# Softmax sums of four heads in one group of matmuls, reciprocals spread by DMA, packed narrow weights, and an output stored batch by batch

## The chip, the cores and the metric

The kernel runs on one core of a Trainium2 chip. Five engines work side by side and meet at semaphores: TensorE (PE), VectorE (DVE), ScalarE (ACT), GpSimd (POOL) and SyncE (SP), which here issues nearly all DMAs. The metric is the time of one execution on the device in microseconds (us); lower is better.

## The reference

Eight layers in a row work on x, 4 batches of 512 tokens with 320 features. In order: a self-attention and a cross-attention with 20 heads of width 64 (inner width 1280) and a gated feed-forward of width 1280; the same three with heads of width 16; a small gated attention; and one more cross-attention with heads of width 16. All is float32. The piece that matters here:

```python
scores = jnp.einsum('bhnd,bhmd->bhnm', q, k) * SCALE
attn = jax.nn.softmax(scores, axis=-1)
out = jnp.einsum('bhnm,bhmd->bhnd', attn, v)
out = out.transpose(0, 2, 1, 3).reshape(B, N, HEADS * DHEAD)
return jnp.einsum('bnf,fe->bne', out, wo) + bo
```

## The kernel before

x stays in SBUF from the first load to the last store. Each engine runs its own instruction list, in program order; what stands on one engine waits for another by semaphores only. The order of work is written out by hand as turns.

**The wide attentions** (`WideRun`, stages 0 and 1) are 8 batches of 10 steps. A step U = 10 n + u handles pair u of heads, two heads of width 64. TensorE computes for it the scores by key block (L491), subtracts the row maxima (L500), computes the bf16 rows of the next step for its maxima (L513), the projections Q and K of the step after the next (`w_QK_first`, `w_QK_rest`, L625 to L635), then `mix` (L574: probabilities times values, the two heads beside each other in 64 columns of the array each) and `den` (L589: the sum of the probabilities over all keys, spread over 64 rows for each head by a stationary block of ones). Before `den`, GpSimd has added the four key blocks of probabilities into `psum` (L556, L560). ScalarE copies `den` out of PSUM into the tile `ox` (L596), VectorE takes the reciprocals in four slices into `rec` (L603) and multiplies the unnormalised output `OT` by it (L609). Every so often a step has more work on TensorE: the output projection `y` of the batch before (L696, u = 1 to 4), the last values `V2` (L679, u = 5 and 6), transposes of the next batch (u = 7), its values (u = 8 and 9). The results of Q, K, y, V, negm, mix and den share two PSUM banks in a fixed rotation: an item waits until the item two places before it was copied out.

SyncE issues in that time the weights of each pair of heads (L907), each after the K projection two steps before.

**The feed-forward** (`ff_pe`) runs over ten column blocks j, and then `out_pe` does four output tiles (L362) in banks 0 and 1 by turns. In its last batch the beginning of the narrow attention (stage 3) is put between those matmuls: its first projection Q0 (L1208) stands in the middle of the second output tile. **Its weights** are loaded by `load_weights` (L220): nine DMAs of one row chunk each, after SyncE has waited on the semaphore `a_ps`, which counts the blocks j done, for all ten of the last batch. Narrow attention works like the wide one, with four heads of 32 columns beside each other (L1083).

**At the end** SyncE waits until the last x is done and stores all of x with one DMA (L2000).

## Time and profile before

| | |
|---|---|
| median of 3 runs | 3449.7 us (3446.83 to 3456.34) |
| the profiled execution | 3453.04 us, of which span 3451.3 us |
| mean granted TensorE clock | 0.987 |
| PE busy | 3262.6 us (95%) |
| DVE, ACT, POOL busy | 1758.6, 1505.9 and 670.5 us (51%, 44%, 19%) |
| DMA | 60.53 MB, mean 18 GB/s |

The span runs from the first to the last instruction; the execution's own time is 1.7 us more. A matmul of 512 float32 columns appears in the trace as two records. Records of matmuls in different parts of the array overlap, and their ends are modelled, so intervals are best read from start to start.

### The profile page before, as it was taken

Reading aid. Unit: us, or ns where it says so; the run is one execution under the profiler, and the core shown is the slowest. Engines: PE = TensorE matmul, PEld = TensorE weight load, DVE = VectorE, ACT = ScalarE, POOL = GpSimd, SP = SyncE. Lnnn points to the kernel's source line nnn. Section 1 sums busy time; section 2 is a strip of 40 time slices with the busy share of each in tenths; the row PEclk is TensorE's granted clock in tenths of the full one; section 3 lists DMA queues with packets and bytes.
Section 4 is the critical chain, followed back from the end, with each engine's and each line's share of the span. In section 5 each row is a group of like instructions: output and inputs, shape, how many; then the busy total and the mean of one; then the engine's idle time right before and its main releaser. Section 6 shows DMA issues by size and latency. Waiting matters only on the chain.

```text
span 3451.3 us, 39291 instructions
## 1 busy us (share of the span) xinstructions
PE 3262.6 (95%) x15478; PEld 1481.0 (43%) x15478; DVE 1758.6 (51%) x2728; ACT 1505.9 (44%) x2023; POOL 670.5 (19%) x420
## 2 busy tenths in 40 slices
PE   7999999999999999999997899999998999989997
PEld 3434344443434344444553344444443555643443
DVE  2645445454545555553222677677772222656774
ACT  3544445445454545451111455666663112326664
POOL 2433334334333434331000000000000000000000
PEclk9999999999999999999999999999999999989999
DMA  3000000000100000000000000000002000000000
GB/s 110 20 16 16 19 16 20 22 15 14 61 13 22 16 19 16 13 29 20 0 1 20 6 1 1 22 1 15 1 22 63 0 0 24 1 5 5 6 1 31
DMA packets 39909, 60.53 MB, mean 18 GB/s; under 512 B 7088, under 2 KB 28336, under 8 KB 39216
## 3 DMA queue, kind: packets, MB, share of 16 engines
q1 hardware_dynamic: 39728, 58.02, 5.7%
q8 instruction: 125, 2.05, 0.2%
q14 instruction: 56, 0.46, 0.0%
HBM read 55.39 MB, written 2.62 MB: 17 GB/s over the span
## 4 chain that ended last, share of the span: by engine, by line
PE 86%; ACT 6%; DVE 5%; issue 1%; DMA 0%; SPq 0%; POOL 0%; ACTq 0%; DVEq 0%; POOLq 0%
PE bank L574 8%; PE bank L491 8%; PE bank L1547 8%; PE bank L1083 6%; PE bank L696 5%; PE bank L362 5%; PE bank L632 5%; PE bank L1016 4%; PE bank L1208 3%; PE bank L635 3%; PE bank L668 3%; PE bank L1233 2%; PE bank L1136 2%; PE bank L513 2%; DVE heads L1041 2%; PE bank L1552 2%
## 5 line engine op out<-in xcount | busy, mean ns | idle before, releaser
L524 DVE TENSOR_REDUCE heads<-bank 128x2 f32<-128x1024 f32 x320 | 392.4, 1226 | 676.5 <-PE bank L513 676.5
L1041 DVE TENSOR_REDUCE heads<-bank 128x1 f32<-128x512 f32 x960 | 598.1, 683 | 238.2 <-PE bank L1029 237.2
L547 ACT ACTIVATE probs<-bank 128x1024 f32<-128x1024 f32 x320 | 327.7, 1024 | 130.1 <-PE bank L500 129.9
L560 POOL TENSOR_TENSOR heads<-heads,probs 128x1024 f32<-128x1024 f32 x160 | 377.2, 2357 | 12.5
L556 POOL TENSOR_TENSOR heads<-probs 128x1024 f32<-128x1024 f32 x80 | 190.6, 2382 | 935.0 <-ACT probs L547 935.0
L491 PE MATMUL bank<-heads 64*128 64x512 f32 x1280 | 335.7, 602 | 0.1
L1016 PE MATMUL bank<-heads 32*128 32x512 f32 x1920 | 296.9, 628 | 25.1 <-ACT weights L1054 10.6
L574 PE MATMUL bank<-probs,values 128*64 128x512 f32 x1280 | 292.3, 598 | 8.9 <-ACT heads L643 4.4
L1547 PE MATMUL bank<-hT,weights 128*128 128x512 f32 x640 | 290.1, 603 | 5.6 <-DVE ysum L378 4.1
L603 DVE RECIPROCAL rec<-ox 128x128 f32<-128x128 f32 x320 | 270.2, 907 | 8.9 <-ACT ox L596 8.9
L1054 ACT ACTIVATE weights<-bank 128x1024 f32<-128x1024 f32 x236 | 228.7, 1022 | 96.0 <-PE bank L1016 94.7
L1029 PE MATMUL bank<-heads 32*128 32x512 bf16 x960 | 214.6, 388 | 26.6 <-DVE heads L1041 7.4
L1610 ACT ACTIVATE ctx_in<-bank,b_col 128x512 f32<-128x512 f32 x80 | 55.0, 687 | 422.9 <-PE bank L1552 327.3
L1226 POOL CAST heads<-heads 128x512 bf16<-128x512 f32 x60 | 35.6, 616 | 865.9 <-ACT heads L1217 865.9
L1629 DVE SCALAR_TENSOR_TENSOR mixed<-bank,b_col,ctx_in 128x512 f32<-128x512 f32 x80 | 60.0, 750 | 265.7 <-ACT ctx_in L1610 151.0
L1547 PEld LDWEIGHTS bank<-hT,weights 128*128 128x128 f32 x640 | 118.3, 191 | 170.7 <-issue 170.2
L1054 ACT ACTIVATE probs<-bank 128x1024 f32<-128x1024 f32 x164 | 158.9, 1021 | 63.1 <-PE bank L1016 62.3
L362 PE MATMUL bank<-weights,mixed 128*128 128x320 f32 x640 | 176.3, 434 | 1.7 <-DVE mixed L1629 1.3
L643 ACT COPY heads<-bank 128x512 f32<-128x512 f32 x160 | 93.5, 584 | 184.5 <-PE bank L632 165.2
L1029 PEld LDWEIGHTS bank<-heads 32*128 32x128 bf16 x960 | 63.7, 92 | 237.3 <-issue 112.3
L632 PE MATMUL bank<-hT,heads 128*128 128x512 f32 x320 | 160.7, 625 | 0.0
L574 PEld LDWEIGHTS bank<-probs,values 128*64 128x64 f32 x1280 | 84.8, 136 | 172.2 <-issue 139.5
(200 smaller groups left out, 4593.2 us busy)
## 6 DMA issues: line engine op xcount, KB each, us to landing
heads<-in_wqk SPq DMA_DIRECT2D x40, 320.0 KB, 2.9
heads<-in_wqk SPq DMA_DIRECT2D x40, 256.0 KB, 2.6
weights<-in_L_xattn_w_ff SPq DMA_DIRECT2D x3, 1600.0 KB, 7.3
weights<-in_L_xattn_ff_w SPq DMA_DIRECT2D x3, 1600.0 KB, 7.3
ctx_in<-in_ctx SPq DMA_DIRECT2D x12, 384.0 KB, 3.7
weights<-in_L_xattn_wo SPq DMA_DIRECT2D x2, 1600.0 KB, 12.0
x_res<-in_x SPq DMA_DIRECT2D x4, 640.0 KB, 12.2
out<-x_res SPq DMA_DIRECT2D x1, 2560.0 KB, 8.7
```

The lines of the kernel that those rows point to most:

```text
L362: last = nc.tensor.matmul(M.PJ[t % 2][:, 0:D], v["OT"][c][:, t * P:t * P + P], v["wo"][:, c, :], start=c == 0, stop=c == NF - 1)
L491: nc.tensor.matmul(cols[:, g, :], v["KT"][strip, U % 2, kb * P:kb * P + P], v["QT"][strip, U % 2, :], start=True, stop=False)
L524: nc.vector.tensor_reduce(v["negm"][:, U % 2, qb, :].rearrange("p (g k) -> p g k", g=2)[:, :, 0], M.ROWS[:, :, :], AX.X, ALU.max, negate=T ...
L547: nc.scalar.activation(v["probs"][:, kb, :, :], M.COLS[kb % 2][:, :, :], ACT.Exp, scale=float(r.work[n][0].prm["dh"]) ** -0.5).then_inc(r. ...
L560: nc.gpsimd.tensor_tensor(ps, ps, pr[:, k, :, :], ALU.add).then_inc(r.sem("part"), 1)
L574: last = nc.tensor.matmul(bank[64 * g:64 * g + 64, :], v["V"][:, kb, 2 * u + g, :], v["probs"][:, kb, g, :], start=kb == 0, stop=kb == TB - 1)
L632: last = nc.tensor.matmul(q[:, :], w[:, e, :], M.hT[:, e, :], start=False, stop=e == 1)
L1016: last = nc.tensor.matmul(M.QUAD[:, g, :], v["KT"][strip, u, kb * P:kb * P + P], v["QT"][strip, u, :], start=True, stop=True)
L1029: nc.tensor.matmul(r.bank_of(item, m)[:, :], v["QB"][strip, u, qb * P:qb * P + P], v["KB"][strip, u, :], start=True, stop=True).then_inc(r ...
L1041: nc.vector.tensor_reduce(v["negm"][:, tile, qb, 32 * h + at:32 * h + at + 1], r.bank_of(item, m)[:, :], AX.X, ALU.max, negate=True).then_ ...
L1054: nc.scalar.activation(v["probs"][g % slots][:, 2 * h:2 * h + 2, :], M.QUAD[:, 2 * h:2 * h + 2, :], ACT.Exp, scale=float(r.work[n][0].prm[ ...
L1547: last = nc.tensor.matmul(bank[:, :], v["w1"][:, j, 2 * part + e, :], M.hT[:, e, :], start=first and e == 0, stop=(not first) and e == 1)
```

## The change

Six things are changed.

1. **`den` once in two steps.** In odd steps four matmuls sum the probabilities of four heads, the even step's two and the odd step's two, each into 32 rows of the bank; in even steps there is no `den`. ScalarE's copy and VectorE's four reciprocals follow once in two steps.
2. **The spread.** The reciprocals of one head then stand in 32 rows, and 64 are wanted. SyncE copies them with eight DMAs of 32 rows for every two steps: four into `ox` (the even step's heads), four into `rec_odd`, a free place in `heads`. VectorE waits for all eight, one step later, and does both multiplications.
3. **y and V2 change places**: y at u = 2 to 5, V2 at u = 0 and 1.
4. **Packed narrow weights.** The host packs wq, wk and wv of a narrow attention into one array of 3264 columns, loaded by one DMA (of more bytes than before, since the chunks are filled up to 128 rows). wo is one DMA instead of three. For stage 3 the load waits until six blocks j of the last feed-forward batch are done, not ten.
5. **Four banks** for the four output tiles of the feed-forward, and no wait for `ysum` between them.
6. **The output** goes out in seven DMAs: one for each of the first three batches, and one for each tile of the last batch, each after its own x is done.

```diff
-                sp.wait_ge(stages[2].sem("a_ps"), after(B - 1, NF, NF))
...
+                sp.wait_ge(stages[2].sem("a_ps"), after(B - 1, NF, 6))
...
-            if s.index in (3, 4, 7):
-                if s.index != 4:
-                    load_columns(sp, s)
-                for name, chunks in (("wq", CH3), ("wk", CCH2 if p["cross"] else CH3), ("wv", CCH2 if p["cross"] else CH3)):
-                    for c, (a, w) in enumerate(chunks):
-                        load(v[name][0:w, c, :], p[name][a:a + w, :])
-                s.n_loads = n
+            if s.index != 4:
+                load_columns(sp, s)
+            sp.dma_start(M.weights[:, 3200:6464], s.prm["wqkv"]).then_inc(s.w_in, 16)
+            s.n_loads = 1
...
-                if t >= 2:
-                    pe.wait_ge(s.sem("ysum"), after(b, TB, t - 1))
                 for c in range(NF):
-                    last = nc.tensor.matmul(M.PJ[t % 2][:, 0:D], v["OT"][c][:, t * P:t * P + P], v["wo"][:, c, :], start=c == 0, stop=c == NF - 1)
+                    last = nc.tensor.matmul(M.bank[t][:, 0:D], v["OT"][c][:, t * P:t * P + P], v["wo"][:, c, :], start=c == 0, stop=c == NF - 1)
...
-                if u in (1, 2, 3, 4) and old:
-                    items += [(f"y{u - 1}", n - 1)]
-                if u in (5, 6) and now:
-                    items += [(f"V2_{2 * u - 10}", n), (f"V2_{2 * u - 9}", n)]
+                if u in (2, 3, 4, 5) and old:
+                    items += [(f"y{u - 2}", n - 1)]
+                if u in (0, 1) and now:
+                    items += [(f"V2_{2 * u}", n), (f"V2_{2 * u + 1}", n)]
...
-                    items += [(f"mix{u}", n), (f"den{u}", n)]
+                    items += [(f"mix{u}", n)] + ([(f"den{u}", n)] if u % 2 else [])
...
-            for g in range(2):
-                last = nc.tensor.matmul(r.bank_of(item, n)[64 * g:64 * g + 64, :], M.ones[:, :], v["psum"][:, U % 2, g, :], start=True, stop=True)
+            for e in range(2):
+                for g in range(2):
+                    at = 64 * g + 32 * e
+                    last = nc.tensor.matmul(r.bank_of(item, n)[at:at + 32, :], M.ones[:, 0:32], v["psum"][:, e, g, :], start=True, stop=True)
...
-            r.wait(act, "rcp", 4 * (10 * n + u))
+            r.wait(act, "on", 10 * n + u - 1)
...
+        def w_recip_dve(dve, r, U):
+
+            for j in range(4):
+                c = slice(j * P, j * P + P)
+                if j == 0:
+                    r.wait_out(dve, f"den{U % 10}", U // 10)
+                    r.wait(dve, "spread", 128 * (U // 2))
+                nc.vector.reciprocal(M.rec[:, c], M.ox[:, c]).then_inc(r.sem("rcp"), 1)
+
+        def w_spread_sync(sp, r, U):
+
+            r.wait(sp, "rcp", 4 * (U // 2 + 1))
+            for e, home in ((0, M.ox), (1, n_view(r, 0)["rec_odd"])):
+                for a in range(0, P, 32):
+                    at = 64 * (a // 64) + 32 * e
+                    sp.dma_start(home[a:a + 32, :], M.rec[at:at + 32, :]).then_inc(r.sem("spread"), 16)
+
+        def w_divide_dve(dve, r, U):
+
+            r.wait(dve, "spread", 128 * (U // 2 + 1))
+            for W, rec in ((U - 1, M.ox), (U, n_view(r, 0)["rec_odd"])):
+                out = n_view(r, W // 10)["OT"][W % SLOTS]
+                r.wait_out(dve, f"mix{W % 10}", W // 10)
+                nc.vector.tensor_tensor(out, out, rec[:, :], ALU.mult).then_inc(r.sem("on"), 1)
...
+                    if u % 2 == 0 and U >= 2:
+                        w_recip_dve(dve, r, U - 1)
+                    if u % 2 and U >= 3:
+                        w_divide_dve(dve, r, U - 2)
...
+                if U % 2 == 0 and U >= 6:
+                    w_spread_sync(sp, r, U - 5)
...
+            for U in (75, 77, 79):
+                w_spread_sync(sp, r, U)
...
+            sp.dma_start(M.weights[:, 2048:3008], s.prm["wo"]).then_inc(s.sem("wo_in"), 16)
...
-            sp.wait_ge(x_done, X_IN + len(stages) * NX)
-            sp.dma_start(io["out"].rearrange("(t p) d -> p t d", p=P), M.x[:, :, :]).then_inc(x_out, 16)
-            sp.wait_ge(x_out, 16)
+            for b, t0, t1 in [(b, 0, TB) for b in range(B - 1)] + [(B - 1, t, t + 1) for t in range(TB)]:
+                sp.wait_ge(x_done, X_IN + (len(stages) - 1) * NX + b * TB + t1)
+                rows = io["out"][b * N + t0 * P:b * N + t1 * P, :]
+                sp.dma_start(rows.rearrange("(t p) d -> p t d", p=P), M.x[:, b * TB + t0:b * TB + t1, :]).then_inc(x_out, 16)
+            sp.wait_ge(x_out, 16 * (B - 1 + TB))
...
+    def chunks(w):
+
+        parts = CH3 if w.shape[0] == D else CCH2
+        out = np.zeros((P, 3, w.shape[1]), w.dtype)
+        for c, (o, n) in enumerate(parts):
+            out[0:n, c] = w[o:o + n]
+        return out.reshape(P, 3 * w.shape[1])
```

On TensorE the end of a step read as follows before, in every step: `mix`, then `den`, then the rows of the step after the next (L513) and the next scores (L491).

```order
L532 MATMUL bank<-ident,heads 128x128 x4
L574 MATMUL bank<-probs,values 64x512 x8
L589 MATMUL bank<-heads,ones 64x512 x2
L513 MATMUL bank<-heads 128x512 x2
L491 MATMUL bank<-heads 128x512 x2
```

After the change an even step ends like this (line numbers are those of the changed kernel: L518 is the negm transpose, L561 mix, L499 the rows, L477 the scores):

```order
L518 MATMUL bank<-ident,heads 128x128 x4
L662 MATMUL bank<-weights,hT 128x512 x2
L670 MATMUL bank<-weights,hT 128x512 x4
L561 MATMUL bank<-probs,values 64x512 x8
L499 MATMUL bank<-heads 128x512 x2
L477 MATMUL bank<-heads 128x512 x2
```

and an odd one like this:

```order
L662 MATMUL bank<-weights,hT 128x512 x2
L670 MATMUL bank<-weights,hT 128x512 x4
L561 MATMUL bank<-probs,values 64x512 x8
L579 MATMUL bank<-heads,ones 32x512 x4
L499 MATMUL bank<-heads 128x512 x2
L477 MATMUL bank<-heads 128x512 x2
```

Two matmuls into 64 rows in each step have become four into 32 rows in every second one (L579); nothing else of the step is missing or new.

On VectorE two steps of the changed kernel, with what each waits for, at u = 2 and 3 of a cross-attention batch (L510 the maxima, L595 the reciprocals, L611 the multiplications, L705 and L708 the output y):

```order
L510 TENSOR_REDUCE heads<-bank4 128x2 [waits r0_rows,r0_full0]
L510 TENSOR_REDUCE heads<-bank4 128x2 [waits r0_rows] x3
L595 RECIPROCAL rec<-ox 128x128 [waits r0_spread,r0_free0]
L595 RECIPROCAL rec<-ox 128x128 x3
L705 TENSOR_TENSOR ysum<-bank7,weights 128x320 [waits s1_gbs1,r0_full1]
L708 TENSOR_TENSOR x_res<-ysum,x_res 128x320 [waits r0_free1]
L879 BN_STATS stats<-x_res 128x6 [waits x_done]
L879 BN_STATS stats<-x_res 128x6 x3
L510 TENSOR_REDUCE heads<-bank4 128x2 [waits r0_rows,r0_full0]
L510 TENSOR_REDUCE heads<-bank4 128x2 [waits r0_rows] x3
L611 TENSOR_TENSOR mixed<-mixed,ox 128x512 [waits r0_free1,r0_spread]
L611 TENSOR_TENSOR mixed<-mixed,heads 128x512 [waits r0_free1]
```

Before, each of the two steps had four reciprocals and one multiplication behind its maxima; now the first has the reciprocals and the second both multiplications, behind a wait for the spread.

On SyncE the spread stands between the loads of pair weights (L908; L603 is the spread). The rows are those around the loads for the feed-forward weights, in the fifth wide batch:

```order
L908 DMA heads<-in_wqk2 128x512 [waits r0_full1] x2
L603 DMA ox<-rec 32x512 [waits r0_rcp]
L603 DMA ox<-rec 32x512 x3
L603 DMA heads<-rec 32x512 x4
L924 DMA weights<-in_L0_xattn_wo2 128x10x320 [waits r0_full1]
L222 DMA g_col<-in_L0_xattn_g3 128x3 [waits r0_free1]
L223 DMA b_col<-in_L0_xattn_be3 128x3
L224 DMA bo_row<-in_L0_xattn_b_ff2 128x320
L225 DMA b1_col<-in_L0_xattn_b_ff1 128x20
L231 DMA weights<-in_L0_xattn_w_ff1 128x3200
L908 DMA heads<-in_wqk2 128x512 [waits r0_full0] x2
L603 DMA ox<-rec 32x512 [waits r0_rcp]
```

There were no DMAs from SBUF to SBUF before; now eight follow every second load of pair weights, and the loads behind them on SyncE wait for their turn.

## Rows read from the trace of the kernel before

**Rows 1.** which stage the time goes to (start:end us, length, busy us of each engine, clock, DMA share, GB/s)

```profile
50.00:1573.00 1523.00, 1473.70 (x6462) 625.32 (x6460) 777.59 (x895) 715.89 (x994) 577.46 (x256) 1.00 0.07 20
...
1850.00:1940.00 90.00, 64.99 (x234) 34.46 (x232) 33.34 (x64) 18.26 (x24) 7.19 (x12) 0.85 0.09 24
```

**Rows 2.** TensorE's timeline in one plain wide step (start us, length us, what, xcount records)

```profile
926.46 3.65 PE L574 MATMUL bank<-probs,values 128*64 128x512 f32 x16
929.95 1.03 PE L589 MATMUL bank<-heads,ones 128*64 128x512 f32 x4
930.91 0.39 PE L513 MATMUL bank<-heads 64*128 64x512 bf16 x2
931.13 1.02 PE L491 MATMUL bank<-heads 64*128 64x512 f32 x4
...
936.93 0.38 PE L513 MATMUL bank<-heads 64*128 64x512 bf16 x2
937.24 1.98 PE L632 MATMUL bank<-hT,heads 128*128 128x512 f32 x4
...
947.15 0.39 PE L513 MATMUL bank<-heads 64*128 64x512 bf16 x2
```

**Rows 3.** TensorE's timeline in the narrow attention, mix of four heads

```profile
3425.96 1.93 PE L1083 MATMUL bank<-weights,values 128*32 128x512 f32 x16 [1.56 <-ACT probs L1054]
3427.68 1.93 PE L1083 MATMUL bank<-probs,values 128*32 128x512 f32 x16
```

**Rows 4.** timeline of VectorE and GpSimd in the wide step of Rows 2 and the next

```profile
937.40 4.79 POOL L560 TENSOR_TENSOR heads<-heads,probs 128x1024 f32<-128x1024 f32 x2
...
938.49 3.38 DVE L603 RECIPROCAL rec<-ox 128x128 f32<-128x128 f32 x4
...
953.59 1.23 DVE L524 TENSOR_REDUCE heads<-bank 128x2 f32<-128x1024 f32 x1 [0.92 <-PE bank L513]
...
963.89 1.23 DVE L524 TENSOR_REDUCE heads<-bank 128x2 f32<-128x1024 f32 x1 [3.71 <-PE bank L513]
```

**Rows 5.** SyncE's queue, timeline (the time is that of issuing, count of DMAs behind)

```profile
1850.70 0.33 SPq L1498 DMA_DIRECT2D g_col<-in_L_xattn_n_g  x1
...
2655.68 3.56 SPq L1963 DMA_DIRECT2D heads<-in_ctx  x8
```

**Rows 6.** DMA issues (count, KB each, median us from issue to landing)

```profile
heads<-in_wqk SPq DMA_DIRECT2D x40, 256.0 KB, 2.6
...
weights<-in_L_xattn_ff_w SPq DMA_DIRECT2D x3, 1600.0 KB, 7.3
...
weights<-in_L_xattn_bo SPq DMA_DIRECT2D x2, 160.0 KB, 5.2
...
heads<-in_ctx SPq DMA_DIRECT2D x8, 12.0 KB, 5.7
```

**Rows 7.** timeline around the end of wide attention, VectorE and TensorE

```profile
1577.78 0.69 DVE L609 TENSOR_TENSOR mixed<-mixed,rec 128x512 f32<-128x512 f32 x1
...
1584.84 2.85 PE L696 MATMUL bank<-weights,heads 128*128 128x320 f32 x10
```

**Rows 8.** waits between 1838 and 1945 us (us in total, times, longest)

```profile
PE bank L1208 <- DMA weights<-in_L_xattn_v: 16.1, 1, 16.1
...
ACT hT L1177 <- DMA heads<-in_L_xattn_o_b: 6.5, 1, 6.5
```

**Rows 9.** timeline of TensorE around the beginning of stage 3

```profile
1828.94 7.13 PE L1547 MATMUL bank<-hT,weights 128*128 128x512 f32 x16
...
1851.75 8.24 PE L362 MATMUL bank<-weights,mixed 128*128 128x320 f32 x30
1876.12 5.49 PE L1208 MATMUL bank<-hT,weights 108*128 108x512 f32 x6 [16.13 <-DMA weights<-in_L_xattn_v]
...
1902.79 2.85 PE L1208 MATMUL bank<-hT,weights 108*128 108x512 f32 x6 [0.77 <-DVE heads L1041]
```

**Rows 10.** timeline of the last microseconds

```profile
3442.14 0.39 SPq L2000 DMA_DIRECT2D out<-x_res  x1
```

More of the change, by code:

```diff
@@ L553, in w_sum_pool @@
             if U >= 2:
-                r.wait_full(pool, f"den{(U - 2) % 10}", (U - 2) // 10)
+                W = U - 1 - U % 2
+                r.wait_full(pool, f"den{W % 10}", W // 10)
             r.wait(pool, "exp", 4 * U + 2)
@@ L781, in wide_pe @@
                         w_QK_rest(pe, r, m, w)
-                    if u in (1, 2, 3, 4) and old:
-                        w_y_pe(pe, r, n - 1, u - 1)
-                    if u in (5, 6) and now:
-                        w_V2_pe(pe, r, n, 2 * u - 10)
-                        w_V2_pe(pe, r, n, 2 * u - 9)
+                    if u in (2, 3, 4, 5) and old:
+                        w_y_pe(pe, r, n - 1, u - 2)
+                    if u in (0, 1) and now:
+                        w_V2_pe(pe, r, n, 2 * u)
+                        w_V2_pe(pe, r, n, 2 * u + 1)
                     if u == 7:
@@ L827, in wide_act @@
                         w_QK_act(act, r, m, w, "K")
-                    if u in (5, 6) and now:
-                        w_V_act(act, r, n, 2 * u - 10, 2)
-                        w_V_act(act, r, n, 2 * u - 9, 2)
+                    if u in (0, 1) and now:
+                        w_V_act(act, r, n, 2 * u, 2)
+                        w_V_act(act, r, n, 2 * u + 1, 2)
                     if u == 7:
@@ L857, in wide_dve @@
                 nc.vector.memset(V[s.name]["wv"][64:P, last_chunk(s), 1024:1280], 0.0).then_inc(r.sem("wv_zero"), 1)
-            def divide(U):
-                for j in range(4):
-                    w_recip_dve(dve, r, U // 10, U % 10, j)
-                w_divide_dve(dve, r, U // 10, U % 10)
             for n in range(-1, r.N):
@@ L869, in wide_dve @@
                         w_rows_dve(dve, r, U + 1, qb)
-                    if U >= 1:
-                        divide(U - 1)
-                    if u in (1, 2, 3, 4) and old:
-                        w_y_dve(dve, r, n - 1, u - 1)
+                    if u % 2 == 0 and U >= 2:
+                        w_recip_dve(dve, r, U - 1)
+                    if u % 2 and U >= 3:
+                        w_divide_dve(dve, r, U - 2)
+                    if u in (2, 3, 4, 5) and old:
+                        w_y_dve(dve, r, n - 1, u - 2)
                     if now:
@@ L889, in wide_dve @@
                                 norm_apply(t, at)
-            divide(10 * r.N - 1)
+            w_recip_dve(dve, r, 10 * r.N - 1)
+            w_divide_dve(dve, r, 10 * r.N - 1)
         def wide_pool(pool, r):
@@ L1133, in y_pe4 @@
             r.wait_out(pe, "out2", n)
-            pe.wait_ge(r.work[n][0].sem("wo_in"), 48)
+            pe.wait_ge(r.work[n][0].sem("wo_in"), 16)
             for c, (a, w) in enumerate(CH3):
@@ L1502, in load_out @@
         def load_out(sp, s):
-            for c, (a, w) in enumerate(CH3):
-                sp.dma_start(V[s.name]["wo"][0:w, c, :], s.prm["wo"][a:a + w, :]).then_inc(s.sem("wo_in"), 16)
+            sp.dma_start(M.weights[:, 2048:3008], s.prm["wo"]).then_inc(s.sem("wo_in"), 16)
         def narrow_sync(sp, r):
@@ L2140, in by_tile, with small @@
         return out.reshape(P, 10 * 5 * P)
+    def chunks(w):
[4 more added lines that the diff above has]
+        return out.reshape(P, 3 * w.shape[1])
+    def small(prefix, wq, wk, wv, wo, **names):
+        packed = [chunks(f(arr(prefix + w))) for f, w in ((repeat_end, wq), (repeat_end, wk), (by_four, wv))]
+        return plain(prefix, **names) | {"wqkv": put(f"in_{prefix}qkv_{wq}", np.concatenate(packed, 1)),
+                                         "wo": put(f"in_{prefix}{wo}", chunks(rows_by_four(arr(prefix + wo))))}
     def plain(prefix, **names):
-        order = {"w1": by_tile, "g": columns, "be": columns, "b1": columns, "wq": repeat_end, "wk": repeat_end}
-        if prefix != L0 and "wq" in names:
-            order |= {"g": thirds, "be": thirds, "wv": by_four, "wo": rows_by_four}
+        order = {"w1": by_tile, "g": columns, "be": columns, "b1": columns}
+        if prefix != L0 and "w1" not in names:
+            order |= {"g": thirds, "be": thirds}
         return {k: put(f"in_{prefix}{v}", order.get(k, lambda a: a)(arr(prefix + v))) for k, v in names.items()}
@@ L2163 @@
         },
-        "L3": plain(L3, wq="Wq", wk="Wk", wv="Wv", wo="Wo", bo="bo"),
+        "L3": small(L3, wq="Wq", wk="Wk", wv="Wv", wo="Wo", bo="bo"),
         "out": nc.dram_tensor("out_0", (B * N, D), F32, kind="ExternalOutput").ap(),
```

32 lines of the change are left out of this document (8 added, 24 removed).

## The prediction

> **What bounds the kernel now.** I read the windows by stage first. In the wide attentions TensorE is busy for 1473.7 of 1523 us, at full clock, while VectorE, ScalarE and GpSimd have half their time free or more [rows 1]. So work taken from TensorE there comes off the time, and work taken from the others doesn't. The one stretch of the table where TensorE is idle for long is 1850 to 1940 us, the start of stage 3: 65.0 of 90 us busy at a mean clock of 0.85 [rows 1]. The waits of that stretch name a load: 16.1 us in one piece for the narrow weights, on TensorE [rows 8]. At the end one DMA stores all of x, with nothing beside it [rows 10]. These are the three places where the change can show. Everything else in it touches engines or queues with time to spare.
>
> **The change part by part.**
>
> *den in every second step.* From the start of den to the next matmul it takes 930.91 - 929.95 = 0.96 us [rows 2]. Two matmuls of 64 columns run abreast in it. The question is whether four of 32 columns run abreast too. The trace has that form in the narrow mix: 16 records from 3425.96 to 3427.68, 1.72 us [rows 3]. In the wide mix 16 records take 929.95 - 926.46 = 3.49 us [rows 2]. So 32 columns go four abreast and 64 go two abreast, and the new den of four matmuls (8 records) should take 8 / 16 x 1.72 = 0.86 us, as long as the old one of two. The 80 dens become 40.
>
> An even step then loses 0.96 us, less whatever the hand-over from mix to the rows costs by itself. That hand-over is in the 0.96 already (den to rows), so I count what is left, 0.86. In an odd step den now follows mix in another column layout. The trace has no pair of exactly these layouts. The nearest is a change in row layout: two bf16 matmuls of 64 partitions that start at 930.91 are followed by others of 64 partitions at 931.13, after 0.22 us, and the same two at 936.93 by one of 128 partitions at 937.24, after 0.31, so about 0.1 us is lost [rows 2]. Within one layout, mix to old den, the loss is 3.49 - 3.44 = 0.05 [rows 2, 3]. I take the new hand-over at 0.04 more than the old one for the sum, and keep 0 and 0.1 (and 0.3, three times the row) as bounds. Gain: 40 x (0.86 - 0.04) = 33 us; bounds 40 x 0.86 = 34 and 40 x (0.86 - 0.3) = 22.
>
> The Trainium skill (TensorEngine Tiling (Array Packing), Key Properties) states that changing the tiling mode drains TensorE. It speaks against this part, since every odd step gets one more change of mode. It names no price; with the 0.1 us of the row above in full the gain would be 30 us instead of 33.
>
> GpSimd isn't late for it: its last addition of that step ends at 937.40 + 4.79 = 942.19, and den starts 0.96 before 947.15, at 946.19 [rows 2, 4]. Den now waits for the same addition of the odd step and for one a step older.
>
> *Copy, reciprocals, multiplications.* 40 copies on ScalarE and 160 reciprocals of 3.38 / 4 us on VectorE go [rows 4]. Neither engine bounds, so I cost this at nothing; what hides it is TensorE's own list.
>
> *The spread.* This is the new wait. Reciprocals end at 938.49 + 3.38 = 941.87 [rows 4]. Eight small DMAs were issued in 3.56 us elsewhere [rows 5]; a load of pair weights of 256 KB lands 2.6 us after its issue, and small ones behind others after 5.7 us [rows 6]. So the last of eight lands 3.6 + 2.6 = 6.2 us after the reciprocals, or 9.3 at the far end. VectorE wants them after its fourth maximum of the next step, 953.59 + 1.23 = 954.82, that is 12.9 us after the reciprocals, about 1 less since den is gone in between [rows 4]. So the wait is normally over before it begins. If it weren't, the first to wait is the multiplication; behind it on VectorE stand the y output, the norm, and the maxima of the step after, which start at 963.89 [rows 4] and for which TensorE waits at once. With 1.7 us for two multiplications the spread may land 963.89 - 1.7 - 941.87 = 20.3 us after the reciprocals, some 17 in the shorter steps without extra work (about 2 less, and den's 1), before TensorE loses anything. Cost: 0. On SyncE the loads of pair weights are queued behind the spread; they are wanted two steps (28 us or more) after their turn, so 9.3 us more leave them hidden. The longest queue is in step 45, in the fifth batch, where 3.2 MB for the feed-forward go ahead of the weights of pair 49, one step later than before, since they wait for the fourth y tile. Two loads of 7.3 us, 3 for issuing and 2.6 for the pair's own [rows 6] make 20. Till the projections that want it in step 47 there are mix (3.5), step 46 (16.2 like the step of rows 2, 14 without its V2) and the 5 us of scores before the projections [rows 2]: 22.5. Hidden, with the least room of all; a us too late costs a us, once.
>
> The Trainium skill (DMA: Bandwidth & Descriptors, Rules for kernel authors) warns that transfers under 64 KB pay mostly overhead, and each of these has 64 KB. By its fit, 2.0 us and the bytes at 436 GB/s, one takes 2.2 us, which agrees with the 2.6 us row and leaves the wait hidden.
>
> *The last spread* has no next step to hide in. Before, the multiplication began at 1577.78, right behind the reciprocals, and the first y matmul that needs it at 1584.84, 7.1 us later [rows 7]. Now come 6.2 us for the spread and two multiplications of 0.7 to 0.9: 7.8 us. Loss 1 us; at the far end (9.3) 4.
>
> *y and V2 exchanged, four banks for the output tiles.* The same matmuls at other places. V2 is needed by mix from u = 8, y's input is ready a step ahead. The rotation of the two banks stays, so each still waits for the item two places before it. Cost 0. Within an output phase TensorE runs 30 records from 1851.75 on in one piece [rows 9], so there is no wait that four banks could remove. Gain 0.
>
> *Narrow weights of stage 3.* Q0 starts at 1876.12 and waited 16.13 us for them [rows 9]. The load is now released when six blocks j are done instead of ten. The sixth ends with the first half of the piece from 1828.94, so at about 1832.5 [rows 9]; before, SyncE began at 1850.70 [rows 5]. With 1.3 us for three columns and 7.3 us for one DMA of 1.6 MB [rows 6] it lands at about 1841, and Q0 would start at 1876.1 - 16.1 = 1860.0. 19 us of room, so the wait goes in full, and ScalarE's wait for the columns (6.5 us, [rows 8]) with it. After the pause TensorE ran at half clock (1.2 instead of 2.4 GHz): 6 records of L1208 take 5.49 us, and 2.85 at full clock a little later [rows 9]. That 2.6 us comes back too, as no pause stands ahead. Gain 16.1 + 2.6 = 18.8 us. Bounds: 14 if the columns or the transposed inputs end the wait instead, 21 if the stretch behind keeps a better clock as well. What is late next in this stretch are the short waits for VectorE's maxima, 0.77 us at 1902.79 [rows 9], which are there already.
>
> *The other packed loads* (stages 4 and 7, wo) caused no wait and are only fewer. 0.
>
> *The output.* The store is issued at 3442.14 and the span ends at 3451.3: 9.2 us for 2560 KB [rows 10]. Now only a tile of 160 KB is left at that point, by the row of 256 KB 2.6 us, and 0.4 for issuing: 3.0. Gain 9.2 - 3.0 = 6.2 us; bounds 3.6 (160 KB behind others took 5.2, [rows 6]) and 7.
>
> **Sum.** 33 - 1 + 18.8 + 6.2 = 57 us. The profiled execution took 3453.0 us, with a span of 3451.3, so it would become 3396. It is 3.3 us over the median of the runs; against the median 3449.7 the forecast is 3449.7 - 57 = **3392.7**. The bounds together: 34 + 21 + 7 = 62 (3388) and 22 - 4 + 14 + 3.6 = 36 (3414).
>
> **The rivals.**
>
> 1. *Four 32-column matmuls run two abreast.* Then the new den takes 1.7 us in every second step and the wide stage gains nothing. Rows 3 speak against it: the same form goes four abreast there. Left: 18.8 + 6.2 - 1 = 24, 3426 us. Chance 4%.
>
> 2. *The spread is late (the other side).* Place: the wait before the two multiplications in each odd step. It decides from 17 us after the reciprocals, where every further us costs up to 40 us in the kernel; with 18.5 us the whole gain of 57 is gone, with 20 the kernel is at 3449.7 - 57 + 120 = 3513. For it: the spread stands on SyncE behind loads that wait on semaphores, so one blocked load would hold it back. Against it: 9.3 us is the most that the rows give. Chance 4%.
>
> 3. *The DMA wait of stage 3 goes, but the stretch is bound by something else*, the lead-in of ScalarE's and VectorE's small steps behind Q0. Then 8 of the 18.8 us come: 3403. Chance 8%. For it: the stretch has such waits already. Against: they stand behind Q0, so they move with it.
>
> 4. *The hand-over between layouts costs more, 0.3 us in every odd step*, and some of den's 0.96 was cover for ScalarE's work at the start of a step: 22 us instead of 33 in the wide stage, 3404. Chance 14%.
>
> **How the numbers follow.** The main forecast holds 70%: 3392.7, its own range 3388 to 3400. Rivals 3 and 4 lie at 3403 and 3404 and are taken into the range; rivals 1 and 2 are left out, with a little of each end. Below, a few us may come from a wait that I count as zero (shorter steps, a better clock at the start of stage 3), so the range begins at 3385. Range 3385 to 3408. A measurement of this kernel tells changes of about 0.3% (10 us) from none. All cases but rival 2 are faster by more: faster 0.94, same 0.02, slower 0.04.
>
> **What would show it.** The den rows should be 320 records of 32 columns, 40 groups, with about 0.86 us from first to next matmul; VectorE should show next to no wait on the spread DMAs except once, at the end of the wide attention; the DMA wait of Q0 should be missing and the clock be full at that point; the last DMA should end some 3 us after its issue. Wrong it would be if a plain even step is shorter by clearly less than 0.86 us, if the multiplications wait on DMAs in steady state, or if TensorE shows new idle time before y, V2 or the pair's projections.

## The result and the profile after

The changed kernel takes 3394.65 us (median of 4, 3393.92 to 3401.26) against 3450.45 us (4 runs, 3446.83 to 3456.34): ratio 0.9841, 95% interval 0.9822 to 0.9859. The forecast was 3392.7 us with a range of 3385 to 3408. The profiled execution has a span of 3391.8 us, so 59.5 us less than before. That is 3.7 us more than the medians' 55.8: the profiled execution before (3453.04 us) lies above its median and the one after (3393.92) is the fastest of its four.

The windows of the wide stage and of the start of stage 3, in the changed kernel:

```profile
core 0: us, PE busy (x) PEld busy (x) DVE busy (x) ACT busy (x) POOL busy (x), PEclk, DMA share, GB/s
50.00:1544.00 1494.00, 1444.07 (x6456) 608.43 (x6456) 754.87 (x734) 691.29 (x954) 593.00 (x256) 1.00 0.13 34
1821.00:1910.00 89.00, 78.14 (x349) 39.61 (x347) 47.85 (x90) 31.58 (x40) 7.17 (x12) 0.94 0.02 6
```

TensorE still bounds the wide stage, and the start of stage 3 has 78.1 of 89 us busy where it had 65.0 of 90 [rows 1]. TensorE's timeline around the end of an even step and of the odd one behind it (L561 is mix, L579 den, L499 the rows):

```profile
908.23 3.65 PE L561 MATMUL bank<-probs,values 128*64 128x512 f32 x16
911.82 0.39 PE L499 MATMUL bank<-heads 64*128 64x512 bf16 x2
...
927.12 3.65 PE L561 MATMUL bank<-probs,values 128*64 128x512 f32 x16
930.70 1.06 PE L579 MATMUL bank<-heads,ones 128*32 128x512 f32 x8
931.70 0.39 PE L499 MATMUL bank<-heads 64*128 64x512 bf16 x2
```

Before, mix to rows took 930.91 - 926.46 = 4.45 us in every step [rows 2]. Now it takes 911.82 - 908.23 = 3.59 in an even step (0.86 less) and 931.70 - 927.12 = 4.58 in an odd one (0.13 more). That is 0.73 us a pair and 29.2 in 40 pairs. The feed-forward's first matmul comes at 1544.47 instead of 1573.58, 29.1 us earlier. Of that 0.8 had been gained by the 22nd us, where the two kernels have the same work; the kernels of the experiments, which begin the same way, lie 0.2 to 1.5 us behind the changed one by 60 us, so I put the 0.8 down to scatter. That leaves 28.3. Added up over all steps, the last one with its wait for GpSimd included, mix to rows has become 28.7 us shorter.

The end of the wide stage, on TensorE and on VectorE:

```profile
1542.61 1.93 PE L579 MATMUL bank<-heads,ones 128*32 128x512 f32 x8 [3.25 <-POOL heads L547]
1544.47 4.29 PE L1551 MATMUL bank<-hT,weights 128*128 128x512 f32 x8
...
1550.60 3.70 PE L1551 MATMUL bank<-hT,weights 128*128 128x512 f32 x8
1556.50 2.93 PE L698 MATMUL bank<-weights,heads 128*128 128x320 f32 x10 [2.19 <-issue]
```

```profile
1536.27 1.23 DVE L611 TENSOR_TENSOR mixed<-mixed,ox 128x512 f32<-128x512 f32 x1 [6.45 <-DMA heads<-rec]
...
1545.27 3.39 DVE L595 RECIPROCAL rec<-ox 128x128 f32<-128x128 f32 x4 [5.00 <-ACT ox L586]
1555.10 0.69 DVE L611 TENSOR_TENSOR mixed<-mixed,ox 128x512 f32<-128x512 f32 x1 [6.45 <-DMA heads<-rec]
```

VectorE stands 6.45 us for the last spread, and y0 (L698) starts 2.19 us late. Against [rows 7] it is 1584.84 - 1556.50 = 28.3 us earlier, so the tail has cost 0.8. Over the whole kernel VectorE waits for spread DMAs only in the last two pairs, which have no maxima of a next step in between. This row of its waits says so, and this row of the DMA issues the price of one transfer (the issues into `ox` read alike) (columns: tensors, queue, count, KB, median us from issue to landing):

```profile
DVE mixed L611 <- DMA heads<-rec: 12.9, 2, 6.5
```

```profile
heads<-rec SPq DMA_DIRECT2D x160, 64.0 KB, 2.0
...
weights<-in_L_xattn_qkv_q SPq DMA_DIRECT2D x2, 1632.0 KB, 7.7
```

Then stage 3. SyncE's queue, and TensorE around the first projection Q0 (L1213):

```profile
1805.44 0.43 SPq L216 DMA_DIRECT2D weights<-in_L_xattn_qkv_q  x1
```

```profile
1823.13 8.24 PE L348 MATMUL bank<-weights,mixed 128*128 128x320 f32 x30
1831.20 2.74 PE L1213 MATMUL bank<-hT,weights 108*128 108x512 f32 x6
...
1843.01 1.88 PE L1264 MATMUL bank<-weights,hT 108*128 108x320 f32 x6 [0.77 <-DVE heads L1046]
```

The load is issued 25.8 us ahead of Q0, the wait is gone, and the clock is full: six records in 2.74 us against 5.49 [rows 9]. Q0 stands 44.9 us earlier than before, so 16.6 more than at y0. The first V matmul (L1264) is 47.8 earlier (its partner before began at 1890.82), 2.9 more: the clock. By the last output projection of the kernel (L1141, 3381.84, before 3434.34) it is 52.5. Of these last 4.7 us 1.4 came later in stage 3 and 2.9 in stage 7, where the stretches at half clock lie otherwise. I don't put the 2.9 down to the change: the first kernel under "The tail" below has the same code there and again takes 3.1 us longer for it than the changed kernel.

The end, by SyncE's queue and VectorE:

```profile
3384.85 5.12 SPq L2006 DMA_DIRECT2D out<-x_res  x4
```

```profile
3389.11 0.49 DVE L1150 TENSOR_TENSOR x_res<-ysum,x_res 128x320 f32<-128x320 f32 x1
```

The last x is done at 3389.60 and the span ends at 3391.8: 2.2 us. Before, it was 9.2 [rows 10].

### The profile page after: what moved, and what is told of

Read it like the earlier page. It is cut to its first block, busy times and chain, and to the rows that moved or that the text cites. A ratio compares the mean times of both kernels' runs of the same rounds, so it can differ in the third digit from the quotient of the medians.

```text
span 3391.8 us, 39231 instructions
## 1 busy us (share of the span) xinstructions
PE 3224.7 (95%) x15478; PEld 1460.9 (43%) x15478; DVE 1735.3 (51%) x2568; ACT 1481.3 (44%) x1983; POOL 685.6 (20%) x420
## 4 chain that ended last, share of the span: by engine, by line
PE 87%; ACT 6%; DVE 5%; issue 2%; POOL 0%; DMA 0%; ACTq 0%; DVEq 0%; POOLq 0%
PE bank L561 8%; PE bank L477 8%; PE bank L1551 8%; PE bank L1088 6%; PE bank L698 5%; PE bank L348 5%; PE bank L634 5%; PE bank L1021 4%; PE bank L1213 3%; PE bank L670 3%; PE bank L637 3%; PE bank L1238 2%; PE bank L1141 2%; PE bank L499 2%; DVE heads L1046 2%; PE bank L1556 2%
## 5 line engine op out<-in xcount | busy, mean ns | idle before, releaser
L510 DVE TENSOR_REDUCE heads<-bank 128x2 f32<-128x1024 f32 x320 | 392.3, 1226 | 663.0 <-PE bank L499 663.0
L547 POOL TENSOR_TENSOR heads<-heads,probs 128x1024 f32<-128x1024 f32 x160 | 389.8, 2436 | 12.5
L477 PE MATMUL bank<-heads 64*128 64x512 f32 x1280 | 335.7, 602 | 0.1
L561 PE MATMUL bank<-probs,values 128*64 128x512 f32 x1280 | 292.3, 598 | 8.9 <-ACT heads L645 4.4
L1551 PE MATMUL bank<-hT,weights 128*128 128x512 f32 x640 | 288.5, 601 | 5.6 <-DVE ysum L364 4.1
L1633 DVE SCALAR_TENSOR_TENSOR mixed<-bank,b_col,ctx_in 128x512 f32<-128x512 f32 x80 | 59.9, 750 | 259.5 <-ACT ctx_in L1614 148.1
L1551 PEld LDWEIGHTS bank<-hT,weights 128*128 128x128 f32 x640 | 117.9, 190 | 169.6 <-issue 169.1
L561 PEld LDWEIGHTS bank<-probs,values 128*64 128x64 f32 x1280 | 84.8, 136 | 172.3 <-issue 141.8
L348 PEld LDWEIGHTS bank<-weights,mixed 128*128 128x128 f32 x640 | 120.5, 190 | 53.0 <-DVE mixed L1633 2.9
```

Of the source, the lines that this page charges most:

```text
L348: last = nc.tensor.matmul(M.bank[t][:, 0:D], v["OT"][c][:, t * P:t * P + P], v["wo"][:, c, :], start=c == 0, stop=c == NF - 1)
L477: nc.tensor.matmul(cols[:, g, :], v["KT"][strip, U % 2, kb * P:kb * P + P], v["QT"][strip, U % 2, :], start=True, stop=False)
L510: nc.vector.tensor_reduce(v["negm"][:, U % 2, qb, :].rearrange("p (g k) -> p g k", g=2)[:, :, 0], M.ROWS[:, :, :], AX.X, ALU.max, negate=T ...
L547: nc.gpsimd.tensor_tensor(ps, ps, pr[:, k, :, :], ALU.add).then_inc(r.sem("part"), 1)
L561: last = nc.tensor.matmul(bank[64 * g:64 * g + 64, :], v["V"][:, kb, 2 * u + g, :], v["probs"][:, kb, g, :], start=kb == 0, stop=kb == TB - 1)
L1551: last = nc.tensor.matmul(bank[:, :], v["w1"][:, j, 2 * part + e, :], M.hT[:, e, :], start=first and e == 0, stop=(not first) and e == 1)
```

## The experiments

Each is the changed kernel with one edit, or two where the heading says so. "Changed" is the median of 3394.65 us or its span of 3391.8; each time is a median of 4 to 10 runs, with a ratio to the kernel before that ran beside it.

### One den in each step, no spread

```diff
-                        if u % 2:
-                            w_den_act(act, r, n, u)
+                        w_den_act(act, r, n, u)
...
-                    if u % 2 == 0 and U >= 2:
-                        w_recip_dve(dve, r, U - 1)
-                    if u % 2 and U >= 3:
-                        w_divide_dve(dve, r, U - 2)
+                    if U >= 1:
+                        divide(U - 1)
```

> The changed kernel with the sums, reciprocals and multiplications of the wide attentions as before: den in every step with two matmuls of 64 columns, no spread; everything else as changed. My theory: pairing the dens is worth 0.86 us in each even step less 0.13 in each odd one, 40 x 0.73 = 29 us, and the spread costs 2.2 us at the end of the wide attention and nothing elsewhere. So 3394.7 + 29 - 2 = 3422 us, and the wide stage from 24 us on takes 27 to 29 us longer. Rival: the gain of the wide stage comes from VectorE and ScalarE having less to do, or from y and V2 in their new places; then this kernel is within 10 us of the changed one.

3421.86 us (3421.4 to 3426.55), ratio 0.9923 (0.9908 to 0.9938): 27.2 above changed. TensorE's timeline shows the old end of a step, and the start of the feed-forward:

```profile
1543.48 3.65 PE L560 MATMUL bank<-probs,values 128*64 128x512 f32 x16
1546.96 1.03 PE L575 MATMUL bank<-heads,ones 128*64 128x512 f32 x4
1547.92 0.39 PE L499 MATMUL bank<-heads 64*128 64x512 bf16 x2
...
1572.90 3.70 PE L1532 MATMUL bank<-hT,weights 128*128 128x512 f32 x8
```

The feed-forward starts at 1572.90 instead of 1544.47, 28.4 us later, and y0 follows at 1581.98 without a wait. So den is 28 of the 56 us, and the other half of the gain is there without it. This kernel also has y and V2 at their new places, and its feed-forward starts only 0.7 us earlier than that of the kernel before (1573.58): the exchange by itself is worth next to nothing.

### Do four matmuls run abreast, and what does the hand-over cost?

The first kernel issues den's four matmuls twice:

```diff
-            for e in range(2):
+            for e in (0, 1, 0, 1):
```

> The changed kernel, with each group of four den matmuls of 32 columns done twice over (eight instead of four, same result). Theory: they go four abreast, so 40 x 0.86 = 34 us more, 3429 us. Rival (two abreast): 69 us more, 3464 us.

3430.2 us (3428.31 to 3435.48), ratio 0.9947. The second kernel keeps the four matmuls but gives each 64 columns; it leaves the sums of the two steps added together:

```diff
-                    at = 64 * g + 32 * e
-                    ... [at:at + 32, :], M.ones[:, 0:32], ..., start=True, stop=True)
+                    at = 64 * g
+                    ... [at:at + 64, :], M.ones[:, :], ..., start=e == 0, stop=e == 1)
```

> The changed kernel, with the four den matmuls writing 64 columns each, the even step's sums added to the odd step's (so each head is divided by the sum of two heads' probabilities; the values differ, the work doesn't). They go two abreast, so the stream takes as long as in the kernel with the den done twice, 34 us over the changed one, but mix and den have the same layout. Theory: the hand-over from 64 to 32 columns costs 0.1 us each, so this is 4 us below the kernel with the den done twice, and in the rows mix to den takes 3.49 us instead of 3.58. Rival: the 0.13 us belong to something else; then both are equal and mix to den stays at 3.58.

3428.42 us (3425.26 to 3433.18), ratio 0.994. TensorE at the same place of a step, first with den twice, then with 64 columns:

```profile
946.58 3.65 PE L561 MATMUL bank<-probs,values 128*64 128x512 f32 x16
950.16 1.92 PE L579 MATMUL bank<-heads,ones 128*32 128x512 f32 x16
952.02 0.39 PE L499 MATMUL bank<-heads 64*128 64x512 bf16 x2
```

```profile
943.20 3.65 PE L561 MATMUL bank<-probs,values 128*64 128x512 f32 x16
946.68 1.89 PE L579 MATMUL bank<-heads,ones 128*64 128x512 f32 x8
948.50 0.39 PE L499 MATMUL bank<-heads 64*128 64x512 bf16 x2
```

Four more matmuls of 32 columns take 1.86 - 1.00 = 0.86 us, the price of two of 64: four run abreast. And with 16 records of 32 columns mix to den takes 3.58 us, with 64 columns 3.48; den to rows 1.86 and 1.82. The change of column layout costs 0.10 us on the way in and 0.04 on the way out, 0.14 x 40 = 5.6 us in the kernel. The two medians differ by 1.8 us where 4 were expected, and the spans (3433.7, 3426.3) by 7.4, so I take the size from the rows.

### The load of stage 3: its release, and its form

First, the packed load but released as late as before; second, nine loads of one row chunk, released early.

```diff
-                sp.wait_ge(stages[2].sem("a_ps"), after(B - 1, NF, 6))
+                sp.wait_ge(stages[2].sem("a_ps"), after(B - 1, NF, NF))
```

> The changed kernel, but the one packed load of stage 3 waits for all ten blocks j again. Theory A (the number and shape of the loads made the 16 us wait): it is issued about 1822 + 1.3 us and lands 7.7 us later, just when Q0 wants it at 1831; cost 0 to 2 us, about 3396 us. Theory B (the late release made it): cost 14 to 19 us, 3409 to 3414 us, with a DMA wait on the first L1213 of 10 us or more.

```diff
-            sp.dma_start(M.weights[:, 3200:6464], s.prm["wqkv"]).then_inc(s.w_in, 16)
-            s.n_loads = 1
+            for name, width in (("wq", 384), ("wk", 384), ("wv", 320)):
+                for c, (_, w) in enumerate(...):
+                    sp.dma_start(V[s.name][name][0:w, c, :], ...).then_inc(s.w_in, 16)
```

> The changed kernel, but the narrow weights come in eight or nine DMAs of one row chunk each, from the packed array, released after six blocks j as in the changed kernel. Before, the nine took 24 us from issue to last landing; released at 1804 they would land at 1829, 2 us before Q0. Theory: no cost (3395 us), since the early release alone covers even the slow loads. Rival: the loads are slower still beside the feed-forward, and Q0 waits up to 5 us.

The packed load released late takes 3397.75 us (3395.61 to 3398.42), ratio 0.9848; nine loads early take 3398.75 us (3393.8 to 3401.18), ratio 0.9851, with a span of 3392.0. SyncE's issue and TensorE's Q0, of the late packed load and then of the nine early ones:

```profile
1823.72 0.43 SPq L216 DMA_DIRECT2D weights<-in_L_xattn_qkv_q  x1
```

```profile
1832.49 2.84 PE L1213 MATMUL bank<-hT,weights 108*128 108x512 f32 x6 [0.80 <-DMA weights<-in_L_xattn_qkv_q]
```

```profile
1805.50 14.24 SPq L219 DMA_DIRECT2D weights<-in_L_xattn_qkv_q  x9
```

```profile
1831.27 2.74 PE L1217 MATMUL bank<-hT,weights 108*128 108x512 f32 x6
```

Released late, the packed load still comes 0.80 us short of in time, where the nine were 16.1 late. Released early, even nine loads that take 14.2 us to issue arrive in time. So each half of the edit alone takes the wait, the packing all but 0.8 us of it; neither is the one cause. The late one has another wait that the early one has not: ScalarE stands 7.3 us for the columns' last piece.

### One store at the end, two output banks

```diff
-            for b, t0, t1 in [...]:
-                sp.wait_ge(x_done, X_IN + (len(stages) - 1) * NX + b * TB + t1)
-                sp.dma_start(rows..., M.x[:, b * TB + t0:b * TB + t1, :])
+            sp.wait_ge(x_done, X_IN + len(stages) * NX)
+            sp.dma_start(io["out"]..., M.x[:, :, :]).then_inc(x_out, 16)
...
-                    ... nc.tensor.matmul(M.bank[t][:, 0:D], ...
+                    ... nc.tensor.matmul(M.PJ[t % 2][:, 0:D], ...
```

> The changed kernel with one store of all of x at the end, and the feed-forward's output tiles in two banks with their wait for ysum. Theory: the end gets 7.0 us longer (9.2 instead of 2.2 us after the last x), the two banks cost nothing: 3401.7 us, and no idle time of L348 by the wait for ysum. Rival: the second wait costs 0.5 us for each of 16 tiles, 8 us more, 3410 us.

3404.44 us (3401.86 to 3405.09), ratio 0.9868. The last x ends at 3394.13 and the span at 3403.3, so 9.2 us again, 7.0 more than in the changed kernel. SyncE's queue has one store:

```profile
3394.16 0.39 SPq L2006 DMA_DIRECT2D out<-x_res  x1
```

TensorE never waits for `ysum` ahead of an output tile of the feed-forward in this kernel, so the two banks cost nothing. The rest of the span's 11.5 us is 4.5: 0.9 are there by 1880 us, 0.5 more come by 2960, and 3.1 come in stage 7, from 3020 us on, by other stretches at half clock, as in the kernel before. What moves these I haven't isolated.

### The spread a step later

```diff
-                if U % 2 == 0 and U >= 6:
-                    w_spread_sync(sp, r, U - 5)
+                if U == 48:
+                    w_spread_sync(sp, r, 43)
+                if U % 2 and U >= 7 and U != 49:
+                    w_spread_sync(sp, r, U - 6)
```

> The changed kernel with each spread one load of pair weights later in SyncE's queue (but for one pair, where that would lock up with the wait for y). SyncE then reaches it about 9 us into the step in which VectorE multiplies, wants it at 7.7, and the last piece lands at about 15.6 us. By the price in the prediction (free until about 17 us after the reciprocals, then us for us) these are 18 to 24 us, so 1 to 7 us for each pair, 40 to 200 us in all. By a closer count only the steps with a y tile are hurt (y's copy stands behind the multiplications, and mix waits for its bank), 2.4 us each in 14 of the 40 odd steps: 34 us, 3430 us. Rival: the spread has no slack at all: every pair loses 8 us, 320 us in all.

3454.05 us (10 runs, 3450.94 to 3457.88), ratio 1.0014 (1.0005 to 1.0024): the whole gain is lost, 59.4 us. The waits of VectorE, of TensorE in the wide stage, and one place of VectorE's timeline:

```profile
DVE mixed L611 <- DMA heads<-rec: 236.1, 27, 10.1
...
DVE heads L611 <- DMA heads<-rec: 98.5, 11, 10.0
```

```profile
PE bank L561 <- DVE ysum L705: 37.6, 13, 3.7
```

```profile
726.15 0.69 DVE L611 TENSOR_TENSOR mixed<-mixed,ox 128x512 f32<-128x512 f32 x1 [9.21 <-DMA heads<-rec]
...
727.37 0.48 DVE L705 TENSOR_TENSOR ysum<-bank,bo_row 128x320 f32<-128x320 f32 x1
```

VectorE stands 335 us, 38 times, yet TensorE loses little of that directly. What waits behind the multiplications is the addition of y (L705), which frees a bank that mix wants: 13 times, 37.6 us. Mix itself then takes 307.3 us for its 1280 records instead of 292.3, since part of it runs at half clock after the pause: 15.0. The waits for maxima grow by 5.4 (5.7 from 0.3). Together these make 58.0 of the 59.4 us by which the feed-forward starts later (1603.89 against 1544.47). So the spread's place in the queue decides, as rival 2 had it, but the first victim is y's bank and not the next maxima. The 13 waits are the late pairs of the steps with a y tile, 2.9 us each where the closer count had 2.4 in 14; the half clock behind them was missing from that count.

How late the spread was can be read too: in 36 of the 40 pairs its last piece lands 18.8 to 31.1 us after the reciprocals (median 23.9). The price of the prediction, free until 17 us and then us for us in each pair, makes 240 us of that. It cost 59.4, and the 23 late pairs without a y tile lost 5.4 us together.

### y and V2 at their old places

```diff
-                    if u in (2, 3, 4, 5) and old:
-                        w_y_pe(pe, r, n - 1, u - 2)
-                    if u in (0, 1) and now:
-                        w_V2_pe(pe, r, n, 2 * u)
+                    if u in (1, 2, 3, 4) and old:
+                        w_y_pe(pe, r, n - 1, u - 1)
+                    if u in (5, 6) and now:
+                        w_V2_pe(pe, r, n, 2 * u - 10)
```

> The changed kernel with y at u = 1 to 4 and V2 at u = 5 and 6, as before the change. y at u = 1 then needs the multiplications of the same step: they end about 9.4 us into it, and TensorE is ready for y at 9.1. Theory: 0.3 to 1 us in each of 7 batches, 2 to 7 us, 3397 to 3402 us. Rival: the multiplications come later in that step and each batch loses 3 us or more.

3421.47 us (3417.38 to 3424.33), ratio 0.9918: 26.8 above changed, nearly all that den in every second step is worth. TensorE's wait row, then one of the seven places on TensorE, on VectorE and on GpSimd:

```profile
PE bank L698 <- issue: 19.0, 7, 3.1
```

```profile
260.53 5.62 PE L698 MATMUL bank<-weights,mixed 128*128 128x320 f32 x20 [2.23 <-issue]
```

```profile
255.86 1.81 DVE L611 TENSOR_TENSOR mixed<-mixed,ox 128x512 f32<-128x512 f32 x1
257.59 2.84 DVE L611 TENSOR_TENSOR mixed<-mixed,heads 128x512 f32<-128x512 f32 x1
```

```profile
254.77 5.11 POOL L547 TENSOR_TENSOR heads<-heads,probs 128x1024 f32<-128x1024 f32 x2
```

The multiplications end at 257.59 + 2.84 = 260.43 and y starts at 260.53, 2.2 us late, in each of seven batches 2.7 on average. My theory put it at 0.3 to 1 because it took the multiplications as short. They aren't: 1.81 and 2.84 us, where the same two take 0.69 each at the end of the stage and where one took 0.84 in the kernel before, behind the reciprocals of [rows 4]:

```profile
941.90 0.84 DVE L609 TENSOR_TENSOR heads<-heads,rec 128x512 f32<-128x512 f32 x1
```

What differs is GpSimd, which is adding then (before, its addition was over at 942.19, 0.29 us after this start); the last section has the same multiplications without it. With 0.69 each, y's input would have stood at 257.2, ahead of TensorE at 258.3. Beside the 19.0 us stand 5.1 in y matmuls that run longer after the pause (640 records in 187.8 us, and in 182.7 in the changed kernel), at half clock after three of the seven. Together they are 24.1 of the 24.4 us by which the feed-forward starts later (1568.92 against 1544.47). So the rival came, 3 us or more for each batch.

### The tail

Two kernels try to take the 2.2 us at y0. The first moves the last four y one block of the feed-forward further back:

```diff
-            if 1 <= j <= 4:
-                w_y_pe(pe, r, r.N - 1, j - 1)
+            for t in {2: (0,), 3: (1,), 4: (2, 3)}.get(j, ()):
+                w_y_pe(pe, r, r.N - 1, t)
```

> The changed kernel with the last wide batch's y tiles one block j later in the feed-forward (after j = 2, 3 and two of them after j = 4). Theory: the 2.2 us in which the first of them waited for the last spread go, all else equal: 3392.5 us, not to be told from the changed kernel by time, but the idle time before the first L698 of the feed-forward is gone. Rival: the two tiles after j = 4 wait for their banks and give it back.

3398.29 us (3397.53 to 3399.15), ratio 0.9852: no gain. The wait only moved, and half clock follows it (5.39 us for 8 records, 3.60 in the changed kernel):

```profile
1557.60 5.39 PE L1551 MATMUL bank<-hT,weights 128*128 128x512 f32 x8 [2.21 <-DVE mixed L1633]
```

Block 2 of the feed-forward waits for the product of block 0 (L1633), and that stands on VectorE behind the multiplication that waits for the spread. The second kernel therefore also puts that product ahead of it:

```diff
-            w_divide_dve(dve, r, 10 * r.N - 1)
...
+                    if b == s.first and r.wide and j == 0:
+                        w_divide_dve(dve, r, 10 * r.N - 1)
                     if b == s.first and r.wide:
                         wide_tail_dve(dve, r, j)
```

> The changed kernel with the last two multiplications of the wide attention put behind the feed-forward's first product on VectorE, and the four y at j = 2, 3, 4, 4. Theory: the 2.2 us at the hand-over are a queue of VectorE behind the last spread; with the product ahead of it neither block j = 2 nor y0 waits, and the time is 2 us below the changed kernel's, 3392 to 3393 us. Rival: the wait goes to the next user of the spread (y0 behind j = 2, or block 3 behind the product of block 1), and the time is that of the changed kernel, 3394 to 3396 us.

```profile
1550.92 0.75 DVE L1632 SCALAR_TENSOR_TENSOR mixed<-bank,b_col,ctx_in 128x512 f32<-128x512 f32 x1 [2.11 <-ACT ctx_in L1613]
1555.25 0.69 DVE L611 TENSOR_TENSOR mixed<-mixed,ox 128x512 f32<-128x512 f32 x1 [3.58 <-DMA heads<-rec]
```

```profile
1559.02 2.96 PE L698 MATMUL bank<-weights,heads 128*128 128x320 f32 x10
```

Neither block 2 nor y0 waits any more, and at block 9 of the feed-forward this kernel is 1611.29 - 1609.15 = 2.1 us ahead of the changed one. Its median is 3393.82 us (3393.11 to 3394.41, ratio 0.9835, 0.982 to 0.985): 0.8 below the changed kernel's and inside its scatter, since the 2.1 us are gone by the last projection: 1.1 of them in stage 3, and 1.5 us with one more stretch at half clock at 2546 us. The cause of the wait is shown; a faster kernel is not.

## Why the prediction was right

**TensorE bounds the wide stage, den is work on it.** Right: 28 us come back with den in every step.

**den +33 us.** The mechanism is right (four abreast, 0.86 us, half as many), the size was 29.2 by the rows and 28.7 over all steps. The step that was off is the hand-over in the odd step: 0.13 us lost instead of 0.04. The 0.1 us that the rows gave as a bound was the better choice, and the rule of the Trainium skill (TensorEngine Tiling (Array Packing), Key Properties: a change of the tiling mode drains TensorE), beside which I had put the gain at 30 us by that bound, agrees with the trace in that the change of layout has a price: 0.14 us is the difference that 64 columns against 32 make here, in and out together. Rival 1 is excluded by the two den experiments, and rival 4 by size: 0.3 us it is not.

**The spread in the steady state, 0.** Right, with no wait in pairs before the last two. Its inputs were 4.9 us of issuing instead of 3.6 and 2.0 us of landing instead of 2.6, together 6.5 by the wait of the last pair, forecast 6.2. The Trainium skill (DMA: Bandwidth & Descriptors, Anatomy of one DMA — SWDGE (gpsimd) path) has 2.0 us and the bytes at 436 GB/s, an estimate of 2.2 us for 64 KB; it gives this for DMAs issued from GpSimd, and the trace shows 2.0 for these of SyncE. Two things were wrong in what I said of a late spread. The two multiplications were to take 1.7 us and take 4.7. And the price of rival 2, from 17 us on for each pair, was about four times too high (240 us by it, 59.4 measured): the first to lose is mix's bank behind y, in 13 steps, not the next maxima in all. Neither mattered at the place where the change puts the spread; a step later the bank behind y decides, and with y at its old place the multiplications do. The weights of the pairs, queued behind the spread, stayed hidden: TensorE never waits for them.

**Last spread -1 us.** -0.8, although the wait is 2.2 us: the matmuls ahead of it ran shorter than before, since less of them fell at half clock (L1551 4.29 us for 8 records). Counted from the end of the reciprocals y0 comes after 7.8 us, as forecast, and before it was 7.1.

**y and V2 exchanged, 0.** Right as a number and wrong as a description. It isn't an exchange of equal places but what keeps the multiplications ahead of y: without it, once the spread is there, 19 us of waits and 27 us in all. The prediction's words that y's input is ready a step ahead are the ones that failed; I had no price for this and no rival.

**Four banks 0, other packed loads 0.** The banks are shown to cost nothing either way; the other loads weren't isolated.

**Stage 3, 18.8 us.** 16.6 and 2.9, so 19.5: right, both the wait and the half clock. Rival 3 (8 us only) falls. The step that named the release as what brings the load forward was half the story: the packing alone would have done 15 of the 16, and the release alone all of it.

**Output 6.2 us.** 7.0, since 160 KB end 2.2 us after the last write, at the upper bound.

**What cancelled.** By marks in the two traces: 29.1 at the feed-forward, -0.8 at y0, 19.5 to the first V matmul, 4.7 from there to the last projection, 7.0 at the end, 59.5 us. By the medians the gain is 55.8 against 57, and the time is 2.0 us above the forecast. That this is so near is in part luck: den gave some 4 us less than its 33, and against that stand 0.8 at the start and 4.7 on the way, which the prediction did not have and most of which isn't the change's doing.

## What to carry to other kernels

Before a hand-over by DMA is called hidden, look at what stands behind the waiting instruction on its engine, and at the duration that instruction has where it will stand, beside its neighbours there. A step's slack is set by the order in which its consumers come: here the exchange of y and V2 was worth nothing alone and, with the spread, as much as the shorter den. When a load is late, count how long its DMAs take to issue before moving its release; one DMA in the place of nine, issued as late as before, took 15 us off.

## What the runs showed of the hardware

VectorE's multiplication of two SBUF tiles of 128 x 512 takes 0.69 us when GpSimd is idle, and 1.81 to 1.87 and 2.83 to 2.86 us when it starts while GpSimd runs its own additions from SBUF. In the changed kernel's steady state, on VectorE and on GpSimd:

```profile
953.07 1.86 DVE L611 TENSOR_TENSOR heads<-heads,ox 128x512 f32<-128x512 f32 x1
954.85 2.84 DVE L611 TENSOR_TENSOR mixed<-mixed,heads 128x512 f32<-128x512 f32 x1
```

```profile
952.03 5.11 POOL L547 TENSOR_TENSOR heads<-heads,probs 128x1024 f32<-128x1024 f32 x2
```

Each multiplication ends 0.55 us after one of GpSimd's additions (the last one ends at 957.14, the multiplication at 957.69), as if it stood until that was over; the maxima, which read PSUM, keep their 1.23 us beside GpSimd. The Trainium skill (SBUF — State Buffer, Who interferes with whom) states this: a VectorE instruction with two SBUF inputs and a GpSimd instruction that reads SBUF share a port, and the one that comes second waits in full. The trace agrees: from 50 to 1530 us the first multiplication of a pair takes 1851 ns on average (38 of them) and the second 2846 (38). The kernel with the spread a step later isolates it, since it moves the multiplications to where GpSimd is idle: 74 of its 80 meet no addition, and each of those takes 0.68 to 0.69 us, as in this row of its L611 (ns, least, median and most):

```profile
L611 DVE TENSOR_TENSOR mixed<-mixed,heads x28: 682/684/2852, 123.1 to 1615.1; 128x512 f32<-128x512 f32 x28
```

A row-chunked load was dear on the issuing side: nine DMAs with 1360 KB took 14.2 us to issue, one packed DMA of 1632 KB 0.43 us, and it landed 8.8 us after its issue in stage 3.
